# Three PSUM banks for the row-maximum products, one for the attention sums, and a transposition three to seven units earlier

## The reference, cut to what matters

```python
h = layernorm(x)
q, k, v = rope(h @ Wq.T), rope(h @ Wk.T), h @ Wv.T          # 16 heads of 16
att = softmax(q @ k.T / sqrt(16))                           # 512 x 512 for each head
x = x + (att @ v) @ Wu.T + bu
h = layernorm(x); hp = h shifted by one token
xr, xk = mu_r * h + (1 - mu_r) * hp, mu_k * h + (1 - mu_k) * hp
x = x + sigmoid(xr @ W_r.T) * (relu(xk @ W_k.T) ** 2 @ W_v.T)
```

## Time and profile before

| | |
|---|---|
| median of 3 runs | 2408.97 us (2403.08 to 2410.29) |
| profiled execution | 2414.42 us, its span 2412.6 us |
| mean granted TensorE clock | 0.958 of full speed |
| PE busy | 2247.4 us (93%) |
| DVE busy | 2036.4 us (84%) |
| ACT busy | 1644.9 us (68%) |
| POOL busy | 1406.3 us (58%) |
| chain that ended last, by engine | PE 33%, POOL 26%, issue 19%, DVE 12%, ACT 4% |

### The profile page before, as it was taken

One profiled execution on the slowest core, in us unless ns is written; L12 is line 12 of the kernel. 1 busy time (PEld: TensorE's weight loads), 2 busy tenths in 40 slices (PEclk: granted clock), 3 DMA queues, 4 the chain that ended last, 5 costly groups with the idle time before them and its releaser, 6 DMA issues.

```text
span 2412.6 us, 48257 instructions
## 1 busy us (share of the span) xinstructions
PE 2247.4 (93%) x13084; PEld 1196.5 (50%) x13084; DVE 2036.4 (84%) x3982; ACT 1644.9 (68%) x3137; POOL 1406.3 (58%) x1184
## 2 busy tenths in 40 slices
PE   5999999999999999999999999999999999999995
PEld 4445445555455455544555454455545555545433
DVE  5778888889888888888988888898889989998862
ACT  2467777767677777767767677676767767777653
POOL 5336765556666565765546765555765646676234
PEclk8789999999999999999999999999999999999977
DMA  6434445544345553344544345553344554444400
GB/s 155 108 88 97 97 89 120 124 105 99 89 87 122 123 119 93 99 101 90 122 113 99 82 93 116 123 122 88 97 104 91 122 125 101 98 92 99 92 28 22
DMA packets 133571, 243.18 MB, mean 101 GB/s; under 512 B 24848, under 2 KB 79760, under 8 KB 120976
## 3 DMA queue, kind: packets, MB, share of 16 engines
q1 hardware_dynamic: 133264, 239.56, 44.0%
HBM read 136.71 MB, written 83.89 MB: 91 GB/s over the span
## 4 chain that ended last, share of the span: by engine, by line
PE 33%; POOL 26%; issue 19%; DVE 12%; ACT 4%; SPq 3%; DMA 2%; DVEq 1%; POOLq 0%; ACTq 0%
PE d_ps L956 13%; PE st_ps L894 9%; POOL f_lo L465 6%; DVE mx L693 5%; PE pv_ps L926 5%; PE s_ps L912 4%; POOL rope_t L415 3%; POOL yn L481 2%; POOL xrT L444 2%; POOL r_lo L451 2%; POOL parts L409 2%; POOL rs L473 2%; POOL parts L425 2%; ACT probs L652 2%; POOL rope_t L418 1%
## 5 line engine op out<-in xcount | busy, mean ns | idle before, releaser
L652 ACT ACTIVATE probs<-st_ps 128x512 f32<-128x512 f32 x2048 | 1155.6, 597 | 624.2 <-PE st_ps L894 617.1
L693 DVE TENSOR_REDUCE mx<-s_ps 128x1 f32<-128x512 f32 x2048 | 1339.0, 678 | 286.0 <-PE s_ps L912 284.9
L912 PE MATMUL s_ps<-k_st,q_st 48*128 48x512 f32 x2048 | 862.6, 480 | 49.6 <-DVE mx L693 42.1
L894 PE MATMUL st_ps<-q_st,k_st 50*128 50x512 f32 x2048 | 820.5, 464 | 62.8 <-issue 30.8
L894 PEld LDWEIGHTS st_ps<-q_st,k_st 50*128 50x128 f32 x2048 | 332.9, 189 | 680.7 <-ACT probs L652 439.9
L926 PE MATMUL pv_ps<-probs,v_ext 128*32 128x512 f32 x4096 | 558.3, 617 | 0.0
L912 PEld LDWEIGHTS s_ps<-k_st,q_st 48*128 48x128 f32 x2048 | 360.3, 189 | 136.4 <-DVE mx L693 122.8
L473 POOL TENSOR_TENSOR rs<-ve,mhalf 128x2 f32<-128x2 f32 x128 | 89.7, 701 | 485.3 <-DVE mean L761 485.3
L465 POOL TENSOR_TENSOR f_lo<-yn,f_hi 128x512 fp32r<-128x512 f32 x128 | 175.0, 1377 | 83.0 <-ACT f_hi L620 83.0
L458 POOL TENSOR_TENSOR f_lo<-attnT,f_hi 128x512 fp32r<-128x512 f32 x64 | 86.2, 1347 | 203.0 <-ACT f_hi L608 202.9
L926 PEld LDWEIGHTS pv_ps<-probs,v_ext 128*32 128x32 f32 x4096 | 81.5, 109 | 167.9 <-issue 164.6
(11 more groups left out here) (118 smaller groups left out, 3988.3 us busy)
## 6 DMA issues: line engine op xcount, KB each, us to landing
parts_scratch<-parts SPq DMA_DIRECT2D x64, 1024.0 KB, 5.4
q_st<-parts_scratch SPq DMA_DIRECT2D x128, 256.0 KB, 6.0
k_st<-parts_scratch SPq DMA_DIRECT2D x128, 256.0 KB, 6.8
xn<-in_L_attn_x_dram SPq DMA_DIRECT2D x32, 512.0 KB, 8.5
q_st<-parts_scratch SPq DMA_DIRECT2D x128, 128.0 KB, 7.4
k_st<-parts_scratch SPq DMA_DIRECT2D x128, 128.0 KB, 7.1
attnT<-attn SPq DMA_DIRECT2D x512, 32.0 KB, 2.0
y<-in_L_attn_x_dram SPq DMA_DIRECT2D x32, 512.0 KB, 5.8
```

Of the source, the lines that this page charges most:

```text
L652: nc.scalar.activation(probs[:, u % SLOTS, j, :], st_ps[:, n % 2, :], ACT.Exp, scale=float(D) ** -0.5).then_inc(exp_done, 1)
L693: nc.vector.tensor_reduce(mx[:, col:col + 1], s_ps[:, n % 2, :], AX.X, ALU.max).then_inc(max_done, 1)
L894: nc.tensor.matmul(st_ps[:, n % 2, :], k_st[par][row:row + SROWS + MROWS, slot, c * P:(c + 1) * P], q_st[par][row:row + SROWS + MROWS, slo ...
L912: nc.tensor.matmul(s_ps[:, n % 2, :], q_st[at][row:row + SROWS, slot, qc * P:(qc + 1) * P], k_st[at][row:row + SROWS, slot, :], start=True ...
```

## The change

`s_ps` gets three banks and `pv_ps` one. The row-maximum products go round the three banks (`ring_bank`; the last of the 64 takes bank 1, so that the next sequence starts again with bank 0), and a product waits for the maximum of the product that last used its bank (`ring_last`): three before it, in one case of 64 two. The first product of a group into the one bank of `pv_ps` waits for stage 0 of the group just before it instead of the one before that. Stage 0 moves from (7,0), (12,0) and (15,0) to (5,0), (9,0) and (13,0): behind the first row maximum of the unit that follows the group's last `values`. That of group 3 stays at (1,0). Stages 1 and 2 stay. `sums` becomes a buffer of its own, and two waits on the shared use fall away. In the code that turns the weights at the start, the seventh uses the third bank of `s_ps`.

```diff
+        sums = sb("sums", [P, T])
-        sums = ynT[:, 0, 1:T + 1]
...
-        s_ps = ctx.enter_context(nc.psum_tensor("s_ps", [P, 2, T], F32))
-        pv_ps = ctx.enter_context(nc.psum_tensor("pv_ps", [P, 2, T], F32))
+        s_ps = ctx.enter_context(nc.psum_tensor("s_ps", [P, 3, T], F32))
+        pv_ps = ctx.enter_context(nc.psum_tensor("pv_ps", [P, 1, T], F32))
...
+        def ring_bank(n):
+
+            return 1 if n == SCORES - 1 else n % 3
+
+        def ring_last(n):
+
+            k = n - 1
+            while ring_bank(k % SCORES) != ring_bank(n):
+                k -= 1
+            return k + 1
...
                 def yT_evac(n):
...
-                        if b.has(NG, 1):
-                            act.wait_ge(attn_done, b.count(NG, 1))
...
-                        nc.vector.tensor_reduce(mx[:, col:col + 1], s_ps[:, n % 2, :], AX.X, ALU.max).then_inc(max_done, 1)
+                        nc.vector.tensor_reduce(mx[:, col:col + 1], s_ps[:, ring_bank(n), :], AX.X, ALU.max).then_inc(max_done, 1)
...
-                        if g == 1 and s.plus(-1).has(4, 4):
-                            dve.wait_ge(shift_done, s.plus(-1).count(4, 4))
-                        nc.vector.transpose(sums, pv_ps[:, g % 2, :]).then_inc(norm_step, 1)
+                        nc.vector.transpose(sums[:, :], pv_ps[:, 0, :]).then_inc(norm_step, 1)
...
-                          (5, 0): [(stats2_of, 0, 0)], (5, 1): [(stats2_of, 0, 1)], (5, 3): [(residual, 1), (split_max, b, 2, 0)],
+                          (5, 0): [(normalise, b, 0, 0), (stats2_of, 0, 0)], (5, 1): [(stats2_of, 0, 1)], (5, 3): [(residual, 1), (split_max, b, 2, 0)],
...
-                          (7, 0): [(normalise, b, 0, 0)], (7, 1): [(normalise, b, 0, 1)],
+                          (7, 1): [(normalise, b, 0, 1)],
...
-                          (8, 3): [(stats1_of, 0, 0)], (9, 1): [(stats1_of, 0, 1)],
+                          (8, 3): [(stats1_of, 0, 0)], (9, 0): [(normalise, b, 1, 0)], (9, 1): [(stats1_of, 0, 1)],
...
-                          (12, 0): [(normalise, b, 1, 0)], (12, 1): [(normalise, b, 1, 1)],
+                          (12, 1): [(normalise, b, 1, 1)],
...
-                          (13, 2): [(split_max, nxt, 0, 0)], (13, 3): [(split_max, nxt, 0, 1)],
+                          (13, 0): [(normalise, b, 2, 0)], (13, 2): [(split_max, nxt, 0, 0)], (13, 3): [(split_max, nxt, 0, 1)],
...
-                          (15, 0): [(normalise, b, 2, 0)], (15, 1): [(normalise, b, 2, 1)],
+                          (15, 1): [(normalise, b, 2, 1)],
...
-                    if s.has(SCORES, n - 1):
-                        pe.wait_ge(max_done, s.count(SCORES, n - 1))
-                    nc.tensor.matmul(s_ps[:, n % 2, :], q_st[at][row:row + SROWS, slot, qc * P:(qc + 1) * P],
+                    if s.has(SCORES, ring_last(n)):
+                        pe.wait_ge(max_done, s.count(SCORES, ring_last(n)))
+                    nc.tensor.matmul(s_ps[:, ring_bank(n), :], q_st[at][row:row + SROWS, slot, qc * P:(qc + 1) * P],
...
-                    if c == 0 and s.has(3 * NG, 3 * g - 5):
-                        pe.wait_ge(norm_step, s.count(3 * NG, 3 * g - 5))
+                    if c == 0 and s.has(3 * NG, 3 * g - 2):
+                        pe.wait_ge(norm_step, s.count(3 * NG, 3 * g - 2))
```

More of the change, by code:

```diff
@@ L210, in weight_bank @@
         def weight_bank(w):
-            return (d_ps, st_ps, s_ps, pv_ps)[w // 2][:, w % 2, :]
+            return (d_ps, st_ps, s_ps)[w // 2][:, w % 2, :] if w < 6 else s_ps[:, 2, :]
         def steps(eng, body, first=FIRST):
@@ L711, in normalise @@
                         return
-                    blocks = sums.rearrange("p (k r) -> p k r", r=32)
+                    blocks = sums[:, :].rearrange("p (k r) -> p k r", r=32)
                     if stage == 0:
@@ L730, in normalise @@
                             dve.wait_ge(attn_in, s.count(64 * NG, 64 * g))
-                        nc.vector.transpose(attn[:, :], sums).then_inc(attn_done, 1)
+                        nc.vector.transpose(attn[:, :], sums[:, :]).then_inc(attn_done, 1)
                 def residual(n):
@@ L842, in step @@
                           (10, 3): [(shift, 0, 0)], (11, 2): [(shift, 0, 1)],
-                          (12, 0): [(normalise, b, 1, 0)], (12, 1): [(normalise, b, 1, 1)],
+                          (12, 1): [(normalise, b, 1, 1)],
                           (12, 3): [(normalise, b, 1, 2)],
-                          (13, 2): [(split_max, nxt, 0, 0)], (13, 3): [(split_max, nxt, 0, 1)],
+                          (13, 0): [(normalise, b, 2, 0)], (13, 2): [(split_max, nxt, 0, 0)], (13, 3): [(split_max, nxt, 0, 1)],
                           (14, 1): [(stats1_of, 1, 0)], (14, 3): [(stats1_of, 1, 1)],
-                          (15, 0): [(normalise, b, 2, 0)], (15, 1): [(normalise, b, 2, 1)],
+                          (15, 1): [(normalise, b, 2, 1)],
                           (15, 3): [(normalise, b, 2, 2)]}
                 if first(b.plus(2)):
-                    extras[5, 0] = [(first_rope, 0), (first_rope, 1), (first_low, 0)]
+                    extras[5, 0] = [(normalise, b, 0, 0), (first_rope, 0), (first_rope, 1), (first_low, 0)]
                     extras[7, 3] = extras.pop((8, 3)) + extras.pop((9, 1)) + extras.pop((14, 1)) + extras.pop((14, 3))
@@ L921, in values @@
                         pe.wait_ge(v_done, s.count(2, 2))
-                    if c == 0 and s.has(3 * NG, 3 * g - 5):
-                        pe.wait_ge(norm_step, s.count(3 * NG, 3 * g - 5))
+                    if c == 0 and s.has(3 * NG, 3 * g - 2):
+                        pe.wait_ge(norm_step, s.count(3 * NG, 3 * g - 2))
                     for j in range(GH):
                         h = head_at(GH * g + j)
-                        ins = nc.tensor.matmul(pv_ps[32 * j:32 * j + 32, g % 2, :], v_ext[half][:, c, VW * h:VW * h + 32],
+                        ins = nc.tensor.matmul(pv_ps[32 * j:32 * j + 32, 0, :], v_ext[half][:, c, VW * h:VW * h + 32],
                                                probs[:, u % SLOTS, j, :], start=(c == 0), stop=(c == TC - 1))
```

## The result

The changed kernel takes 2384.62 us (median of 4 runs, 2382.33 to 2388.87) where the kernel before takes 2407.44: a ratio of 0.9898, 95% interval 0.9871 to 0.9926. Run again later it gave 0.9919 (0.9889 to 0.9949). The gain is some 19 to 23 us, not the 9.9 forecast, and the first measurement lies just under the predicted range.

A forecast was written before the change was run, and what follows sets the result against it. PE and DVE were taken to wait for each other through two banks. +0.63 - 0.45 = +0.18 at Q1 and -0.31 at R0 gave 32 x -0.31 = -9.9 us: 2404.5 profiled, 2399 as median, range 2385 to 2417.

The forecast's parts named there:

- The third bank: Row-maximum products in units 2, 7, 10 and 12: PE's waits for a free bank shrink, as far as other gates allow.
- -0.31 at R0: Unit 12: with most of its 1.06 us stall gone, R0 comes 0.31 us earlier, then waits for POOL's `r_lo`.
- Unit 2's 0: Unit 2: the product could go 0.6 to 0.9 us earlier, but (4,0) waits for DMAs behind `attn`, so nothing is gained.
- The transposition in (5,0): +0.63: DVE's queue ahead of `residual(1)`, without idle time: the moved transposition makes Q0 0.63 us later.
- Unit 7: Product (7,1) waits 0.52 us for a maximum; three banks give back 0.45 of it.
- The transposition in (9,0): 0: DVE in front of (9,2): 0.66 us of idle time hides the transposition's 0.63, so it costs 0.
- FK0: Unit 10's gate, which needs POOL's second `f_lo`: FK0 comes 0.12 us earlier than now, as it can't pass POOL.
- Rival 3: Slower: the transposition in (9,0) isn't hidden and delays `shift`, `f_lo` and `r_lo`; in full +0.32 a step, 2419; chance 0.13.
- R0 to the next Q0: Units 13 to 15, 0 and 1: no product waits for a bank of `s_ps`, so nothing to win, all shifts with R0.
- POOL's collisions: +-0.3 a step: POOL's durations when DVE's instructions move: +-0.3 us a step in the range, for one SBUF collision more or less.
- The clock, left to the range: Behind unit 12's stall a few steps have a clock drop; up to 1.1 us more there, not in the sum.
- Rival 4: Slower: PE stands still before R0 up to 0.7 us and clock drops follow; +7 if every second step, +25 if every; chance 0.08.

The follow-up runs named there:

- e1: The changed kernel with the row-maximum products back on two banks, all else of the change kept: 2426.95 us, ratio 1.0055 to the kernel before.
- e7: The changed kernel with two banks each for products and pv and group 1's transposition back in (12,0): 2419.37 us, ratio 1.0049 to the kernel before.
- e3: The changed kernel with group 1's transposition behind the layer-norm-1 statistics of (9,1) instead of in (9,0): 2371.39 us, ratio 0.9822 to the kernel before.
- e6: The kernel before with one edit, group 2's transposition in (13,0) instead of (15,0): 2399.72 us, ratio 0.9963 to the kernel before.

## Why the prediction missed

The sum of -9.9 us a run was too small by 13. Two of its terms were wrong, one each way, and the clock, which it left to the range, gave the rest. By its own steps:

- **The third bank.** From +0.63 at Q0 to -0.31 at R0 the prediction gives it 0.94 us a step. Measured, where `mean` takes 0.16 us on both sides: 0.84. Against e1: 0.6 to 1.1 a step between steps of one kind without a drop, 32 us in the last column, 33 to 38 in the time. Right in size. Unit 2's 0 was right too: (4,0) waits 0.71 us for the maxima's DMAs, and the waits for `q_st<-mparts` rose to 26.8, a little short of the 30 that were forecast. The row-maximum waits fell to 41.8 (forecast: under 40).
- **The transposition in (5,0): +0.63.** Measured +0.64 at Q0, +0.60 a step in e7. Unit 7 gave back some 0.5 (forecast 0.45).
- **The transposition in (9,0): 0.** This step failed. It was right for the kind of step that was read: `shift` comes 0.03 later there. But it rests on 0.66 us of idle time in front of (9,2), which 13 of the 28 steps of the same trace don't have, because `mean` takes 1.08 us in them. In that kind of step the transposition and the longer `ve` move `shift` by 0.77. Between the two steps set side by side above, which are of different kinds, `shift` came 1.18 later, FK0 0.88 later where 0.12 earlier was forecast, R0 0.76 later where 0.31 earlier was. Rival 3 had the place, but I priced it at the 0.63 of the transposition alone, less an idle time of 0.66 that I took for that of every step. I had looked for collisions at instructions with two SBUF inputs only, and `ve` and `mean` have one. e3, which takes the transposition out from in front of them, gives 13 us in the last column.
- **R0 to the next Q0: "there is nothing to win and all shifts with R0".** This step failed too. I asked only whether products wait for banks there, and not what the transposition taken out of (15,0) holds up. It held up the last maxima, and with them TensorE's arrival at the jump. e6, that move alone, measures it: -9 us (4 to 14 by the interval), 6 in the last column. The sum had no term for it, and the pause of 30.8 us was among the waits of the run.
- **POOL's collisions: +-0.3 a step.** From `shift` to the end of `r_lo` GpSimd takes as long as before (14.0 us in the two steps), though `r_lo(0)` takes 1.8 us instead of 1.3 and `r_lo(1)` 1.26 instead of 1.47. This part of the range wasn't used.
- **The clock, left to the range.** The mean granted clock over the runs is 0.9605 to 0.9631 for the kernel before on three chips, 0.9657 and 0.9692 for the changed one. At 2400 us that is 6 to 21 us, 8 of them (89.8 to 82.0 us lost) where both ran on the same chip. Rival 4's drops in front of R0 came in two steps only (16 and 29, in unit 13), not in every second one. The five behind unit 12 are gone, but e1's zero shows that this needs no third bank. How much of the clock the bank gives stays open.

Together, in the last column of the table: group 2 early -6, group 0 early +18, group 1 early and one bank for pv +11, the third bank -32, from 2317 to 2308. Each was measured on top of the one before it and is good to some 3 to 4 us. The clock gives the rest of the gain, 8 of the 19 us on one chip, and why it rose isn't shown. So "faster" came true, but not by the sum. In the undisturbed steps in which `mean` takes 0.16 us the change gives some 0.2 of the forecast 0.31; in the others, the greater part, it loses 0.4 to 0.5; and what it gains over the run lies mostly at the jump and in the clock. The direction was in part luck: without the jump's 6 us and the clock's 8 (on one chip) some 5 of the 19 are left, less than the 7 that a measurement can tell from no change.

## What to carry to other kernels

An idle time that is to hide something has to be there in every step, not only in the one that was read: here it was missing in 13 of 28, because an instruction in front of it takes 0.16 us or 1.08. When an instruction is moved in an engine's queue, price what it pushes as well: the short instructions behind it may land under a neighbour that locks them out. Compare a step after only with a step before of the same kind. Look at the end of the loop body as at a stage of its own: whatever the last instructions of the busiest engine wait for also decides how much of the jump is hidden. And a gate seen once (GpSimd's `r_lo` in front of R0) is worth an attempt at its own queue: swapping two instructions there gave as much as the whole change.

## What the runs showed of the hardware

- TensorE's sequencer spends 3.3 to 4.0 us in the jump back of this loop, and 1.5 to 2.9 us of it are visible, depending on whether it starts 0.3 us ahead of the last unit's third `score_T` or 0.4 behind it.
- A `tensor_scalar` of 128 x 2 elements takes 0.16 us alone. Started within 0.03 us of a GpSimd difference of 1.04 us, it takes 0.16 or 1.08, in changing shares of the steps of one execution (11 to 24 of 28 in the twelve traces). A transposition out of PSUM takes 0.72 beside such differences, as it does alone (0.71).
- TensorE's mean granted clock of one kernel varies between its runs (0.953 to 0.968 for the kernel before), and the time with it, by 26 us on one chip (2403.91 to 2429.86). Two single executions are compared well only with their clocks beside them.
